# A graph network on one core: the one-hots of the sources go from VectorE to GpSimd while the adjacency is built

## The reference, cut to what matters

```python
src, dst = (edge_index[0], edge_index[1])
agg = jax.ops.segment_sum(x[src], dst, num_segments=n)
h = (1.0 + eps) * x + agg
h = jax.nn.relu(layer_norm(h @ W1, ln_g, ln_b))
```

## Time and profile before

| | |
|---|---|
| median of 3 runs | 2361.07 us (2360.67 to 2363.16) |
| the profiled execution | 2366.88 us, span 2365.1 us |
| the adjacency's windows | 155 to 475 us of the span, 25 tiles |
| in that stretch: VectorE busy | 306.56 of 320 us |
| TensorE busy | 273.27 us, granted clock 0.99 |
| ScalarE, GpSimd busy | 174.52, 26.25 us |

### The profile page before, as it was taken

How to read it: one execution, slowest core, us unless ns; L and a number is a source line. 1 busy time by engine, 2 the same in 40 slices (tenths; PEclk the granted TensorE clock), 3 DMA queues, 4 the chain that set the end, 5 groups by cost and what they waited for, 6 DMA issues and landing times. The chain is left out here.

```text
span 2365.1 us, 41463 instructions
## 1 busy us (share of the span) xinstructions
PE 1997.1 (84%) x12047; PEld 1624.9 (69%) x12047; DVE 1474.2 (62%) x3791; ACT 1036.3 (44%) x1835; POOL 551.5 (23%) x612
## 2 busy tenths in 40 slices
PE   6938888878877758998697898769999965999998
PEld 3526666656633447998365776569888854999997
DVE  3479999978832655554565322399999656444443
ACT  3525555545511524665351343166666430333332
POOL 1000000047611734554310000000000001454443
PEclk9979999977898559999798999989999956999999
DMA  2014334330077301221502342212121081633332
GB/s 69 0 46 133 117 121 129 109 93 1 1 168 211 103 25 54 71 71 54 127 0 54 95 136 63 56 42 65 53 66 53 0 291 54 195 79 75 49 47 33
DMA packets 90653, 189.74 MB, mean 80 GB/s; under 512 B 14121, under 2 KB 58432, under 8 KB 90570
## 3 DMA queue, kind: packets, MB, share of 16 engines
q1 hardware_dynamic: 72906, 157.31, 23.0%
q0 software_dynamic: 17664, 31.47, 6.4%
HBM read 124.22 MB, written 64.52 MB: 80 GB/s over the span
## 5 line engine op out<-in xcount | busy, mean ns | idle before, releaser
L2224 PEld LDWEIGHTS experts_ps_h<-experts_xt,experts_up 128*128 128x128 f32 x2944 | 351.8, 194 | 10.3 <-issue 3.3
L2224 PE MATMUL experts_ps_h<-experts_xt,experts_up 128*128 128x128 f32 x2944 | 353.0, 277 | 3.0 <-DVE experts_xt L2346 1.8
L2851 PE MATMUL gat_ps_o<-Y,gat_prob_t 125*125 125x256 f32 x1250 | 273.9, 379 | 0.0
L2851 PEld LDWEIGHTS gat_ps_o<-Y,gat_prob_t 125*125 125x125 f32 x1250 | 232.7, 188 | 33.7
L1233 PE MATMUL adj_ps_w<-adj_one_k,adj_one_s 128*125 128x500 bf16 x1000 | 178.8, 305 | 78.6 <-DVE adj_one_k L1164 56.0
L2236 PE MATMUL experts_ps_o<-experts_down,experts_hid 128*128 128x256 f32 x960 | 226.7, 379 | 0.0
L2284 ACT ACTIVATE experts_down<-down 128x1024 f32 (+1 forms) x120 | 138.8, 1157 | 175.7 <-DVE experts_out L2334 77.1
L2316 DVE COPY experts_up<-up 128x1024 f32 (+1 forms) x184 | 123.1, 698 | 112.8 <-issue 68.8
L1233 PEld LDWEIGHTS adj_ps_w<-adj_one_k,adj_one_s 128*125 128x125 bf16 x1000 | 98.3, 138 | 128.6 <-DVE adj_one_k L1164 60.2
L2236 PEld LDWEIGHTS experts_ps_o<-experts_down,experts_hid 128*128 128x128 f32 x960 | 173.2, 190 | 18.7
L1177 ACT ACTIVATE adj_tile<-adj_ps_w 125x500 bf16<-125x500 f32 x250 | 95.8, 438 | 150.1 <-PE adj_ps_w L1233 150.1
(11 more groups left out here) (436 smaller groups left out, 3783.9 us busy)
## 6 DMA issues: line engine op xcount, KB each, us to landing
adjacency<-adj_tile SPq DMA_DIRECT2D x25, 683.6 KB
adjacency_t<-adj_tile_t SPq DMA_DIRECT2D x25, 683.6 KB
adj_in<-adjacency_t SPq DMA_DIRECT2D x25, 683.6 KB
QT<-adjacency SPq DMA_DIRECT2D x25, 683.6 KB
cnt<-adjacency_t SPq DMA_DIRECT2D x25, 683.6 KB
up<-in_L_ffn_w SPq DMA_DIRECT2D x32, 512.0 KB, 6.3
down<-in_L_ffn_w SPq DMA_DIRECT2D x16, 512.0 KB, 7.1
up<-in_L_ffn_W SPq DMA_DIRECT2D x8, 512.0 KB, 6.2
```

The lines of the kernel that those rows point to most:

```text
L2224: last = nc.tensor.matmul(ps[:, h * 128:(h + 1) * 128], w[:, k * H + h * 128:k * H + (h + 1) * 128], xt[b][:, k, :], start=(k == 0), stop= ...
L2851: last = nc.tensor.matmul(ps_o[b][0:ROWS, 0:C], prob_t[:, s * ROWS:(s + 1) * ROWS], K.Y[:, s, :], start=(s == 0), stop=(s == TILES - 1))
```

## The change

The four one-hots of the sources of a window are made by GpSimd: it loads the window's first chunk into a register, waits for `win_done`, copies the four columns of source numbers into a small tile `low_here`, drains its engine, and compares the row 0..124 with each of the four columns (four TENSOR_SCALAR of 125 columns). The last one raises a new semaphore, `sources`, for which TensorE waits before a window. VectorE's instruction of 500 columns goes. GpSimd's `sums` of a tile stand behind the comparisons for the next tile. One semaphore more is armed in the stage before.

```diff
-            def sums(t, b, i):
+            def sums(t, b):
...
-            two_by_two(pool, TILES, sums)
+            pool.wait_ge(table_ready, 1 + START)
+
+            def hots(t, b, i, w):
+                win, half = t * WPT + w, (b * WPT + w) % 2
+                first = pool.value_load(table[:, bass.ds(win, 1)], min_val=0, max_val=CHUNKS)
+                pool.wait_ge(win_done, win + 1 + START)
+                nc.gpsimd.tensor_copy(low_here[half][:], low_all[:, bass.ds(first, FIXED)])
+                pool.drain()
+                for j in range(FIXED):
+                    last = nc.gpsimd.tensor_scalar(one_s[half][:, j, :], K.number_row[:, 0:ROWS],
+                                                   low_here[half][:, j:j + 1], None, ALU.is_equal)
+                last.then_inc(sources, 1)
+
+            def ahead(t, b, i):
+                for w in range(WPT):
+                    hots(t, b, i, w)
+
+            ahead(0, 0, 0)
+            with pool.Fori(0, TILES // 2) as i:
+                ahead(i * 2 + 1, 1, i)
+                sums(i * 2, 0)
+                ahead(i * 2 + 2, 0, i + 1)
+                sums(i * 2 + 1, 1)
+            sums(TILES - 1, 0)
...
-                    v.tensor_tensor(one_s[half][:], K.number_row[:, None, 0:ROWS].to_broadcast((CH, FIXED, ROWS)),
-                                    low_all[:, bass.ds(first, FIXED)][:, :, None].to_broadcast((CH, FIXED, ROWS)),
-                                    ALU.is_equal)
                     dve.wait_ge(keyed, win + 1 + START)
...
                 pe.wait_ge(win_read, (win if w == 0 else win - 1) + START)
+                pe.wait_ge(sources, win + 1 + START)
                 fixed(0, True, False)
```

More of the change, by code:

```diff
@@ L51 @@
 BANKS = (range(152, 200), range(200, 248))
-FRONT_SEMS, ADJ_SEMS, MIX_SEMS, UP_SEMS, ROUTE_SEMS, EXPERTS_SEMS, TAIL1_SEMS, GCN_SEMS, PROJECT_SEMS, GAT_SEMS, SETTLE_SEMS = 25, 35, 48, 12, 26, 30, 14, 10, 15, 16, 48
+FRONT_SEMS, ADJ_SEMS, MIX_SEMS, UP_SEMS, ROUTE_SEMS, EXPERTS_SEMS, TAIL1_SEMS, GCN_SEMS, PROJECT_SEMS, GAT_SEMS, SETTLE_SEMS = 25, 36, 48, 12, 26, 30, 14, 10, 15, 16, 48
 LN_EPS = 1e-5
@@ L1013, in build_adjacency @@
         more_ready, more_used = ([m.sem(n + str(i)) for i in range(2)] for n in ("more_ready", "more_used"))
+        sources = m.sem("sources")
+        low_here = [m.sb(f"low_here{i}", (CH, FIXED)) for i in range(2)]
         keyed, one_ready, win_done, win_read, t_done, t_read, stored, t_stored, tile_used = (
```

## The result

The changed kernel takes 2485.1 us (median of 4 runs, 2483.19 to 2487.81) beside 2361.18 before: a ratio of 1.0524, 95% interval 1.0506 to 1.0542. The forecast was 2344.5. The profiled execution took 2483.57 us, its span 116.7 us more than the span of before.

A forecast was written before the change was run, and what follows sets the result against it. VectorE was taken as the adjacency stage's full engine, TensorE nearly full. With VectorE at 11.6 and GpSimd at 11.0, TensorE's 11.85 plus 0.26 gave 12.11 a tile, saving 16.5 us: median 2344.5, forecast range 2338 to 2356 (chance 0.50).

The forecast's parts named there:

- I take 0.14, a little above them for the column's scalar: Column time of one 125-column GpSimd comparison: 0.14 us, between 0.105 from a copy and 0.265 from two-input work.
- GpSimd's tile: 11.0: GpSimd's work per tile in the adjacency stage: five windows of 1.92 plus sums of 1.37, 11.0 us (7.9 to 13.5).
- What GpSimd costs VectorE: Delay of VectorE's one_k beside GpSimd's comparisons: 0.07 us for each comparison (0.035 to 0.195).
- my rule: A comparison shuts VectorE out for its columns and 0.06 us, of which 0.13 between one_k instructions costs nothing.
- The rival built on it: GpSimd shuts VectorE out for each comparison's whole duration, 0.38 us: a tile of 17.8, time 2486; chance 0.04.
- slow comparison: Rival: the comparison passes columns more slowly, at 0.265 us VectorE's tile is 14.1 and the time 2394; chance 0.25.
- The rest is even ... at the start: No further gain or loss: TensorE's new wait is one register instruction, and GpSimd's first window waits for the same table.
- The loading of the register I put at nothing: GpSimd's register load per window, 0.31 us on VectorE's queue, was taken as covered by 1.44 us of comparisons.
- 0.26 late: Window 0's one-hots, made behind the sums, come 0.26 us after TensorE could start, once a tile.
- TensorE's 11.85: TensorE's tile in the adjacency stage without its waits for one_k: 11.85 us in place of 12.77.
- the 23 us: Most the stage could fall: TensorE's waits for one_k after the start, 23.0 us in 26 times, 0.92 a tile.
- wrong if GpSimd is busy through the whole tile: Sign against the forecast in the adjacency stage, where GpSimd was put at 11.0 us a tile, under TensorE's 11.85.

The follow-up runs named there:

- e1_forms: The kernel before, with nine kinds of GpSimd instruction, four of each, added at its start where VectorE is idle; a comparison of 125 columns took 603 ns.
- e13_copies: The changed kernel with four GpSimd copies of 125 columns in place of the four comparisons, same order and waits: 2365.98 us, one run.
- e2_unread: The kernel before plus two GpSimd comparisons per window that nobody reads, VectorE still making all one-hots: 2378.22 us, ratio 1.007.
- e11_none_early: The kernel before with no engine making the four one-hots and VectorE's register loads for windows 0, 1 and 2 at the tile's start: 2344.65 us, one run.
- e14_subtract: The changed kernel with four two-input GpSimd subtractions in place of the four comparisons: 2383.26 us, one run.

## Why the prediction was wrong, step by step

**The step that failed: "I take 0.14, a little above them for the column's scalar", with 0.265 as the upper end.** 125 columns cost 0.31 us (`e1_forms`), outside both bounds. Copy and select, which I chose as nearest because they have one input, are other forms, and the one row of the comparison's own form had six columns. This one-input instruction with a scalar (TENSOR_SCALAR) costs three times a copy's column, 2.5 ns against 0.84, and more than the two-input form's 2.12. My fixed part, 0.24, was near (0.28). The spacing is 2.35 / 4 = 0.59 alone and 0.66 beside VectorE, not 0.33 and 0.36.

**GpSimd's tile: 11.0, measured 17.6.** By the groups above: comparisons 332.3 / 25 = 13.3 (predicted 7.2); copies and the drains behind them, (26.4 + 28.1 - 7.3) / 25 = 1.9 (2.4); sums with their wait about 1.2 (1.4); idle ahead of the copies 30.4 / 25 = 1.2 (none), half of it for TensorE (15.6 us, windows 2 and 3) and half for the register load (14.8 us, window 0). 6.1 of the 6.6 are the price. That copies in the same place brought 119 of 124 us back (`e13_copies`) bears it out.

**What GpSimd costs VectorE: right in size, wrong in rule.** 0.07 predicted, 0.059 measured (`e2_unread`). But by my rule (the columns shut VectorE out, 0.13 are free) 0.31 would have cost it 0.24. VectorE must have gone on while the comparison passed most of its columns; how the two take turns no run shows. The Trainium skill's sentence (SBUF — State Buffer, Who interferes with whom: beside a VectorE instruction in a two-port mode, whoever issues first has the shared pair for the whole instruction) is not what the comparison and `one_k` show: 0.6 us of the one cost the other 0.059. No run shows which mode `one_k` was in. The rival built on it gave 2486, the measured time, by luck: it wanted 0.38 from VectorE for each comparison, and VectorE in fact had time left. A right number does not prove its story.

**The rival "slow comparison" priced the wrong engine.** It let VectorE's tile grow to 14.1; the engine that became the bound was GpSimd, whose upper end I had at 13.5 by the same too low 0.265. The estimate from the Trainium skill's figure for such loops (GPSIMD Engine Reference, Performance pitfalls for Q7 kernels), 0.21 us, was nearer than mine and still too low; the measurement, 0.31, decides.

**"The rest is even ... at the start": wrong by 6 us.** TensorE's first window began at 161.4, before at 155.5. GpSimd in order of time at the start of the stage, and its configuration instructions (min, median, max ns, first and last start):

```profile
151.53 0.19 POOL L1093 COPY adj_low_here<-adj_low 128x4 f32 x1 [4.71 <-DVE adj_table L1166]
158.99 2.35 POOL L1096 TENSOR_SCALAR adj_one_s<-number_row,adj_low_here 128x125 bf16<-128x125 f16 x4 [7.26 <-issue]
```

```profile
L1096 POOLq MODIFY_POOL_CONFIG  x2: 11/11/11, 151.9 to 152.0; - x2
```

Between that instruction and the first comparison lie 7 us. The same gap was in the trace of before (configuration at 177.3, first sum at 184.27), where GpSimd had been idle for 36 us and nobody waited. In `e13_copies`, whose copies need no such change, it moved to the first sum (7.87 us, once), and TensorE stood for 7.78 us there; so the copies did not save it. The Trainium skill (GPSIMD Engine Reference, Instruction dispatch) has about 6 us for the first call to newly loaded code, with no instruction to show for it; the trace fits that, with 7.26, but does not show what fills the gap.

**"The loading of the register I put at nothing": right in four windows of five.** Behind the sums it is 1.13 us long with nothing to cover it (`e13_copies`), and in the changed kernel it is the 14.8 us above. The "0.26 late" ahead of window 0 was 1.0 (1.92 in place of 0.94) even with the copy's lower price.

**TensorE's 11.85: near, and out of reach.** 11.92 was reached, but only without any `one_s` and with the loads moved (`e11_none_early`); without `one_s` alone it is 12.26. So at most 14 of the 23 us were there for this change.

**Right:** `key_here` to the first `one_k` takes 0.26 (357.98 to 358.24; 0.32 predicted); the wait for `one_k` went; VectorE's busy time in the stage fell, from 306.56 to 282.35. My mark "wrong if GpSimd is busy through the whole tile" is what the profile shows. ScalarE's wait of 0.94, which I expected to stay, did not: with GpSimd later still, 3.2 us of it were left in the stage.

**Open:** why a register load takes three to four times as long just behind the stores, and whether VectorE's loads can be had for less. Moved together they cost more than apart; a place that neither bunches them nor meets the stores was not found.

## What to carry to other kernels

Before work goes to an engine, time one instruction of the exact form there, alone; a bound from "near" forms is no bound, and the engine that takes the work needs its own sum with the dear end in it. Then walk through the seam of the loop: what stands ahead of the new instructions in that queue (here the sums, a register load and, once, 7 us behind a change of configuration) costs nothing in the old kernel and holds up the new one. And where a wait names an engine that had long finished, look at the waiting engine's own queue.

## What was not expected of the hardware

- On GpSimd a comparison or multiplication of one input with a scalar costs 2.5 ns a column (`e1_forms`), a two-input one 2.12, a copy 0.84.
- Beside a full VectorE a comparison takes 0.80 us in place of 0.60, and VectorE loses 0.06 (`e2_unread`). Beside shorter subtractions its `one_k` takes 475 ns in place of 376 (`e14_subtract`).
- A load of one register takes 0.3 us. In the kernel before, 47 of VectorE's 125 take 0.5 to 1.4, and they are the ones that start 0.5 to 1.75 us behind the issue of a store. A load of five takes 1.18 on VectorE and 2.58 on GpSimd (medians).
- GpSimd's first comparison or sum of the stage came 7 to 8 us after a change of its configuration, once; its copies did not wait for one.
